# Experts from the second on: transposing the gathered rows by 32x32 blocks on VectorE after a shuffle by transfers, in place of TensorE transposes

## The reference

```python
gates = softmax(x_flat @ gating_w)                      # x_flat: 4096 x 256
topk_w, topk_idx = top_k(gates, 2)
norm_w = topk_w / (sum(topk_w) + 1e-8)
# each expert takes at most 1280 (token, choice) items, in order of tokens
buf[e, slot] = x_flat[token]                            # 8 x 1280 x 256
h = relu(einsum('ecd,edh->ech', buf, w1) + b1)          # hidden width 1024
out_e = einsum('ech,ehd->ecd', h, w2) + b2
out[token] += out_e[e, slot] * norm_w                   # for the items with a slot
x = layernorm(x + out)
```

## Time and profile before

| | us |
|---|---|
| median of 3 runs | 818.93 (818.16 to 819.34) |
| the profiled execution | 819.39 |
| its span, first to last instruction | 817.7 |
| TensorE busy (matmul) | 771.9 (94%) |
| VectorE busy | 605.5 (74%) |
| ScalarE busy | 442.8 (54%) |
| GpSimd busy | 403.4 (49%) |

### The profile page before, as it was taken

One profiled execution on the slowest core, in us unless ns is written; L12 is line 12 of the kernel. 1 busy time (PEld: TensorE's weight loads), 2 busy tenths in 40 slices (PEclk: granted clock), 3 DMA queues, 4 the chain that ended last, 5 costly groups with the idle time before them and its releaser, 6 DMA issues.

```text
span 817.7 us, 16633 instructions
## 1 busy us (share of the span) xinstructions
PE 771.9 (94%) x5919; PEld 644.4 (79%) x5919; DVE 605.5 (74%) x1325; ACT 442.8 (54%) x753; POOL 403.4 (49%) x599
## 2 busy tenths in 40 slices
PE   7789999999999988889999999999999999999993
PEld 6567777777777755778898898888988988988993
DVE  6657888889888898968657568568568567575982
ACT  3156777777777767645345345345445344444670
POOL 1000166665565547764364464463552553546774
PEclk9689999999999999999999999999999999999998
DMA  5567776565555682443352452452441633434841
GB/s 160 119 158 168 173 167 137 138 149 122 121 123 110 126 197 64 160 147 81 83 106 44 97 110 40 97 110 40 101 107 30 150 53 78 103 52 66 316 167 48
DMA packets 71534, 94.35 MB, mean 115 GB/s; under 512 B 10924, under 2 KB 55885, under 8 KB 71324
## 3 DMA queue, kind: packets, MB, share of 16 engines
q1 hardware_dynamic: 53308, 69.10, 32.1%
q0 software_dynamic: 16928, 22.61, 15.6%
q10 hardware_dynamic: 1216, 1.57, 0.9%
HBM read 39.76 MB, written 27.92 MB: 83 GB/s over the span
## 4 chain that ended last, share of the span: by engine, by line
PE 76%; DVE 12%; issue 4%; POOL 3%; DMA 3%; ACTq 0%; ACT 0%; POOLq 0%; DVEq 0%; SPq 0%
PE bank L1723 15%; PE bank L990 11%; DVE negm L895 10%; PE wide L1692 8%; PE wide L1691 8%; PE wide L1690 8%; PE bank L1725 8%; PE wide L1035 7%; PE bank L1669 2%; PE wide L1053 2%; PE bank L999 2%; PE bank L1100 1%; POOL slot_list L538 1%; DMA stack<-qk 1%; POOL out L1420 1%
## 5 line engine op out<-in xcount | busy, mean ns | idle before, releaser
L1364 POOL DMA_INDIRECT acc_rows<-o_w,lists x70 | 116.8, 1668 | 178.7 <-ACT o_w L1513 165.3
L895 DVE TENSOR_REDUCE negm<-wide 128x4 f32<-128x1024 f32 x128 | 156.1, 1222 | 36.8 <-PE wide L1035 36.7
L635 ACT ACTIVATE probs<-wide 128x1024 f32<-128x1024 f32 x128 | 131.0, 1024 | 61.8 <-PE wide L1053 60.2
L1480 ACT ACTIVATE h<-wide,b1T 128x512 f32<-128x512 f32 (+1 forms) x200 | 115.3, 601 | 89.2 <-PE wide L1692 65.2
L1725 PE MATMUL bank<-stack,h_lo 128*128 128x256 f32 x560 | 156.7, 280 | 0.0
L1690 PE MATMUL wide<-g_hi,stack 128*128 128x512 f32 (+1 forms) x400 | 139.4, 349 | 0.9 <-ACT h L1480 0.7
L1692 PE MATMUL wide<-g_hi,stack 128*128 128x512 f32 (+1 forms) x400 | 139.1, 348 | 0.0
L1691 PE MATMUL wide<-g_lo,stack 128*128 128x512 f32 (+1 forms) x400 | 138.9, 347 | 0.0
L1513 ACT ACTIVATE o_w<-o_b,lists 128x256 f32<-128x256 f32 x70 | 35.7, 510 | 147.5 <-DVE o_b L1651 147.5
L1723 PE MATMUL bank<-stack,h_hi 128*128 128x512 f32 x304 | 108.0, 399 | 1.6 <-DVE o_b L1651 1.6
L1725 PEld LDWEIGHTS bank<-stack,h_lo 128*128 128x128 f32 x560 | 105.9, 189 | 0.0
(11 more groups left out here) (212 smaller groups left out, 1637.9 us busy)
## 6 DMA issues: line engine op xcount, KB each, us to landing
stack<-qk SPq DMA_DIRECT2D x180, 128.0 KB, 3.9
w_raw<-in_L_ffn_w SPq DMA_DIRECT2D x16, 1024.0 KB, 5.9
x_sb<-in_L_attn_x SPq DMA_DIRECT2D x16, 256.0 KB, 4.7
x_rows<-x SPq DMA_DIRECT2D x16, 256.0 KB, 3.6
acc_rows<-x SPq DMA_DIRECT2D x16, 256.0 KB, 4.1
acc_sb<-acc_rows SPq DMA_DIRECT2D x8, 512.0 KB, 8.3
out<-acc_sb SPq DMA_DIRECT2D x8, 512.0 KB, 2.6
x_rows<-zrow SPq DMA_DIRECT2D x2, 1152.0 KB, 6.6
```

What stands on the lines that cost most here:

```text
L635: nc.scalar.activation(probs[:, i % 4].rearrange("p x c t -> p x (c t)"), shifted_banks(i)[:, :, :], ACT.Exp, scale=SCALE).then_inc(exp_do ...
L895: nc.vector.tensor_reduce(negm[n % 2][:, :, :, u].rearrange("p c x -> p x c"), score_banks(PAIRS * n + u)[:, :, :].rearrange("p x (c t) -> ...
L1364: nc.gpsimd.indirect_dma_start(out=acc_d, out_offset=bass.IndirectOffsetOnAxis(ap=lists[:, e, QC * c + r, 0:1], axis=0), in_=o_w[c][:, r, ...
L1480: ins = nc.scalar.activation(h[u % 2][:, t], banks[BZ[u % 4]][:, t], ACT.Relu, bias=b1T[:, FT * e + f:FT * e + f + 1])
```

## The change

From expert 1 on, TensorE transposes nothing. The rows of a group are first shuffled from SBUF to SBUF by 16 transfers that SP issues: the transfer (q, t) takes the 32 partitions of token block t, and of each row the 32 columns of column block q out of every 128, and puts them on the 32 partitions of block q. VectorE then turns all 32x32 blocks of a chunk in one transpose instruction (`turn`), and the copy into `g_hi` and the subtraction for `g_lo` read its result from SBUF. The 256 or 128 pieces of a transfer are of 128 bytes each.

SP's program now has, for each expert, the w2 load, the first and the second shuffle, the w1 load of the next expert, and the third shuffle. A shuffle waits for the gathers of its chunks and for the turning of the group two before it. A gather waits for the shuffle that last read its buffer. `AHEAD` goes from 5 to 6. In `expert_order` the taking in moves: chunks 0 and 1 after 5 of the 8 units of the third group's layer 1, chunk 2 after 4 of the 8 units of the first group's, chunks 3 and 4 between layer 2 of chunk 3 and of chunk 4 of the expert before (in the last expert, after layer 1 of its second group). To find room, part of `acc_sb` moves into the weights' raw buffers, and some semaphores are merged. Core of the diff:

```diff
-    AHEAD = 5
+    AHEAD = 6
+    BLOCK = 32
+    QUARTERS = P // BLOCK
+    MOVES = QUARTERS * QUARTERS
+    IN_WEIGHTS = 2
...
+        shuffled = [sb(f"shuffled{i}", [P, PAIR, QC * DK, QUARTERS, BLOCK]) for i in range(2)]
+        turned_rows = [sb(f"turned{i}", [P, QC * DK, P]) for i in range(2)]
...
+        def acc_group(i):
+            if i < 2 * IN_WEIGHTS:
+                raw = (w1_raw, w2_raw)[i // IN_WEIGHTS][:, :, :].rearrange("p x y -> p (x y)")
+                return raw.rearrange("p (i t d) -> p i t d", i=IN_WEIGHTS, t=GROUP)[:, i % IN_WEIGHTS]
+            return acc_sb[:, i - 2 * IN_WEIGHTS]
+        def moved_count(e, s):
+            return 16 * MOVES * ((super_no(e, s) - len(SUPERS)) // 2 + 1)
...
         def sync_program(sp):
-            for e in range(1, NE):
-                sp.wait_ge(gT_ready, NC * (e - 1) + 3)
+            def load_w1(e):
                 sp.wait_ge(w1_hi_done, PARTS * e)
                 sp.wait_ge(w1_lo_done, PARTS * e)
                 sp.dma_start(w1_raw[:, :, :], w1_d[e].rearrange("(c p) f -> p c f", p=P)).then_inc(w1_loaded, 16)
+            def load_w2(e):
                 sp.wait_ge(w2_hi_done, PARTS * e)
                 sp.wait_ge(w2_lo_done, PARTS * e)
                 sp.dma_start(w2_raw[:, :, :], w2_d[e].rearrange("(f p) d -> p f d", p=P)).then_inc(w2_loaded, 16)
+            def shuffle(e, s):
+                i, count = super_no(e, s), len(SUPERS[s])
+                for c in SUPERS[s]:
+                    sp.wait_ge(gathered[c], 16 * QC * (e + 1))
+                if i >= len(SUPERS) + 2:
+                    e_, s_ = divmod(i - 2, len(SUPERS))
+                    sp.wait_ge(turned, NC * (e_ - 1) + SUPERS[s_][-1] + 1)
+                src = rows_of[s][:, :, :, :].rearrange("p c r (k q b) -> p (c r k) q b", q=QUARTERS, b=BLOCK)
+                dst = shuffled[i % 2][:, 0:count].rearrange("p c x t b -> p (c x) t b")
+                for q, t in itertools.product(range(QUARTERS), repeat=2):
+                    sp.dma_start(dst[q * BLOCK:(q + 1) * BLOCK, :, t, :], src[t * BLOCK:(t + 1) * BLOCK, :, q, :]).then_inc(moved[i % 2], 16)
+            sp.wait_ge(gT_ready, 3)
+            load_w1(1)
+            for e in range(1, NE):
+                load_w2(e)
+                shuffle(e, 0)
+                shuffle(e, 1)
+                if e + 1 < NE:
+                    load_w1(e + 1)
+                shuffle(e, 2)
...
             def rows_hi(e, c):
                 s, off = of_chunk(c)
                 i = super_no(e, s)
-                act.wait_ge(gT_ready, NC * e + c + 1)
                 if i >= 2:
                     act.wait_ge(z_ready, unit_no(*divmod(i - 1, len(SUPERS)), 0, None))
+                if e > 0:
+                    act.wait_ge(turned, NC * (e - 1) + c + 1)
+                    nc.scalar.activation(chunk_view(g_hi, e, c), turned_view(e, c), ACT.Copy).then_inc(g_hi_done, 1)
+                    return
+                act.wait_ge(gT_ready, c + 1)
...
+            def turn(e, c):
+                s, off = of_chunk(c)
+                i, n = super_no(e, s), NC * (e - 1) + c
+                dve.wait_ge(moved[i % 2], moved_count(e, s))
+                if n >= 2:
+                    dve.wait_ge(g_hi_done, NC + n - 1)
+                    dve.wait_ge(g_lo_done, NC + n - 1)
+                nc.vector.transpose(turned_rows[(NC * e + c) % 2][:, :, :].rearrange("p x t -> p (x t)"),
+                                    shuffled[i % 2][:, off // C].rearrange("p x t b -> p (x t b)")).then_inc(turned, 1)
+            def take_in(e, chunks):
+                if e > 0:
+                    for c in chunks:
+                        turn(e, c)
+                for c in chunks:
+                    rows_lo(e, c)
...
@@ expert_order
         else:
             layer1(e, second)
-            take_in(e, 3)
-            take_in(e, 4)
+            if last:
+                take_in(e, (3, 4))
             layer2(e, 0)
             layer2(e, 1)
...
+        layer1(e, third, range(5))
+        take_in(e + 1, (0, 1))
+        layer1(e, third, range(5, 8))
+        if split_w1:
+            split_w1(e + 1)
         layer2(e, 2)
         if e + 1 < NE - 1:
-            layer1(e + 1, first)
-            take_in(e + 1, 2)
+            layer1(e + 1, first, range(4))
+            take_in(e + 1, (2,))
+            layer1(e + 1, first, range(4, 8))
         layer2(e, 3)
+        if e + 1 < NE - 1:
+            take_in(e + 1, (3, 4))
         layer2(e, 4)
-        if not last and split_w2:
+        if split_w2:
             split_w2(e + 1)
```

More of the change, by code:

```diff
@@ L119, in _ @@
         def _(pool):
-            gather, add_back = second[1](pool)
+            gather, add_back, rows_free = second[1](pool)
             first[1](pool, gather)
-            second[2](pool, gather, add_back)
+            second[2](pool, gather, add_back, rows_free)
         @block.scalar
@@ L1028, in scores @@
                     pe.wait_ge(wog_lo_done, 1)
[L1029 removed]
+                    pe.wait_ge(gate_copied, 2)
                 pe.wait_ge(max_done, max(i - 1, 0) if i < ALONE else i)
@@ L1232, in experts @@
         lists = sb("lists", [P, NE, BLK, ENTRY_WORDS], I32)
-        rows = [sb(f"rows{c}", [P, QC, D]) for c in range(2)]
+        rows_first = sb("rows_first", [P, 2, QC, D])
         h = [sb(f"h{i}", [P, WIDE]) for i in range(2)]
@@ L1236, in experts @@
         o_w = [sb(f"o_w{c}", [P, QC, D]) for c in range(NC)]
-        rows.append(sb("rows2", [P, QC, D]))
+        rows_second = sb("rows_second", [P, 1, QC, D])
         b2_all = sb("b2_all", [P, NE, D])
         g["b2_all"] = b2_all
-        rows += [sb(f"rows{c}", [P, QC, D]) for c in range(3, NC)]
+        rows_third = sb("rows_third", [P, 2, QC, D])
+        rows_of = (rows_first, rows_second, rows_third)
+        rows = [rows_of[s][:, i] for s, cs in enumerate(SUPERS) for i in range(len(cs))]
         low = [sb(f"low{r}", [P, D]) for r in range(QC)]
@@ L1366, in add_back, with gpsimd_program @@
                         in_=o_w[c][:, r, :], in_offset=None, compute_op=ALU.add).then_inc(added[c], 16)
-            return gather, add_back
-        def gpsimd_program(pool, gather, add_back):
+            return gather, add_back, rows_free
+        def gpsimd_program(pool, gather, add_back, rows_free):
             pool.wait_ge(g["late0_loaded"], 16)
-            for n in range(EC, AHEAD):
-                gather(n // NC, n % NC)
+            for c in range(EC, NC):
+                gather(0, c)
             pool.wait_ge(lists_loaded, 16)
             pool.wait_ge(late_loaded, 16)
+            for n in range(NC, AHEAD):
+                gather(n // NC, n % NC)
             def gather_sums(c):
-                pool.wait_ge(gT_ready, NC * LASTE + c + 1)
+                rows_free(LASTE, c)
                 for i in range(NC):
@@ L1730, in tensor_program, with take_in @@
         def tensor_program(pe, transposes, layer1, layer2):
-            expert_order(NE, transposes, layer1, layer2, None, None)
+            def take_in(e, chunks):
+                if e == 0:
+                    for c in chunks:
+                        transposes(0, c)
+            expert_order(NE, take_in, layer1, layer2, None, None)
         return (sync_program, gpsimd_steps, gpsimd_program, scalar_steps, scalar_program, vector_steps, vector_program,
```

101 lines of the change are left out of this document (60 added, 41 removed).

## The result

The changed kernel takes 841.81 us (median of 4 runs, 838.25 to 842.73), the kernel before 819.13 us on the same chip (818.16 to 820.72): a ratio of 1.0267, interval 1.0231 to 1.0302. The forecast was 827.6 us. The direction was right, the size was not: +22.7 us instead of +8.7. The profiled run takes 842.73 us with a span of 841.0.

The account below looks back on a forecast made before the run. TensorE was taken to bound the kernel, waiting for nothing in the experts. Six waits of 4.0 us less 15.3 us of transposes gave +8.7 us: 828.1 on the profiled run, 827.6 in terms of the median; range 804 to 844.

Parts of the forecast that it names:

- rival D: At layer 2 of chunk 0, each 2.9 us pause also costs 3.5 us of clock: 842 us; 0.20 with rival E.
- What the change takes away: 140 TensorE transposes in experts 1 to 7, 0.109 us each: 15.3 us less, an expert becomes 55.6 us.
- VectorE's and ScalarE's new work: One VectorE turn per chunk at 0.69 us, subtraction 0.69 as before; ScalarE's copy 0.65 us.
- rival E: VectorE's turn costs 1.22 us, total about 840, or 0.43 us, about 823; chance 0.20 together with rival D.
- The third shuffle: Lands at 39.9, for experts 1 to 6; TensorE waits 2.9 us at layer 2 of chunk 0, six times.
- B: Third shuffle hidden, at 0.38 us per transfer; only the 15.3 us saving remains: 803.6 us; chance 0.19.
- C: Third shuffle's burst goes at 0.50 us per transfer and lands 1.7 us late, six times: 813.8 us; chance 0.16.
- The 1.1 us for chunk 0's bank: TensorE wants the bank at 52.9, VectorE's chunk 0 bias ends at 54.0: 1.1 us more, six times.
- The wait for w1's split at 16.5: Before layer 1 of the next expert's first group, w1's first half is 0.1 us late, costed at nothing.
- The first shuffle has cover: It lands near 4.8, its turn comes at 9.0; with the later weighing about 2 us are left, no cost.
- The bias step that ends 1.2 us later: Chunk 2's bias on VectorE ends at 19.6 instead of 18.4, moving the add-back from 18.2 to 19.5.
- The closing stage at nothing: Shared buffers and merged semaphores in the closing stage cost nothing, hidden by layers 1 and 2 of expert 7.

Follow-up runs that it names:

- after: The changed kernel itself, with the whole change made to the kernel before: 841.81 us, ratio 1.0267.
- run 5: Against the changed kernel, TensorE again transposes chunks 0 and 1 of expert 1: 836.25 us.
- both of 6: Two runs against the changed kernel: expert 7's turns of chunks 3 and 4 moved forward, 843.86 us; expert 7's chunks transposed by TensorE again, 836.70 us.
- the first run of 6: Against the changed kernel, expert 7's turns of chunks 3 and 4 moved behind layer 1 of its first group: 843.86 us.
- run 7's second step: Changed kernel with AHEAD 7, TensorE transposing expert 1's chunks 0, 1 and expert 7's 3, 4; plus layer 2 moved earlier between experts 6 and 7: 806.41 us.

## Why the prediction was right and where it failed

The measured 841.8 us lies in the stated range, which was drawn around all the cases, and next to rival D's 842. That is luck: D reaches 842 with 3.5 us of work lost to the clock behind each of six pauses. In the profiled run the clock stayed full behind two of the six and took 1.7 us of work behind each of four; 11 us more come from what D, like the forecast, had at nothing: the closing part (6.2), a second pause in the first period (2.9) and the last period (1.9).

**What the change takes away**: right. 55.62 us where nothing is late, against 55.6.

**VectorE's and ScalarE's new work**: right. Lines of after (busy us, mean ns, idle before):

```profile
L1627 DVE STREAM_TRANSPOSE turned<-shuffled 128x512 f32<-128x512 f32 x35 | 23.2, 693 | 42.8 <-DMA shuffled<-rows_third 37.9 <-DMA shuffled<-rows_first 4.9
...
L1537 ACT ACTIVATE g_hi<-turned 128x512 fp32r<-128x512 f32 x35 | 21.6, 632 | 73.7 <-DVE turned L1627 62.1 <-PE wide L1785 11.5
```

0.693 against 0.69 and 0.632 against 0.65; rival E is out. The pace in the Trainium skill's "Vector Engine (DVE) Microarchitecture Reference", section 3.8, had given an estimate near 0.6 us; the measurement decides for 0.69.

**The third shuffle**: right in place and size: six pauses of 3.0 us in the mean against 2.9. From the first issue to the turn it is 13.1 us in the period shown, against 12.3, and the gather before it lands 0.4 earlier. B and C, which need 0.38 and 0.50 us an issue, are out: the bursts shown take 10.3 to 11.4 us for 16, and the one that holds the period shown takes 0.71 an issue, more than the 0.644 charged. The shuffle of the second group, with half the bytes and half the pieces, takes 10.26 where the first takes 10.52 (run 5's fence). So what is paid for is neither bytes nor pieces: back to back a transfer costs 0.65 us. The Trainium skill's "DMA: Bandwidth & Descriptors", Rules for kernel authors, has transfers under 64 KB pay mostly overhead, and these two bursts agree.

**The 1.1 us for chunk 0's bank**: mis-sized. It is 0.4 in each of the two periods with full clock, and nothing in the other three, in which the lower clock stretches the products and VectorE is in time. The wait for w1's split at 16.5, where no margin was left, came in two of the five and was 0.3 and 0.2 us.

**The clock**: put at nothing in the forecast, and at 3.5 us of work per pause in rival D; both are wrong. In after the clock stays full behind two of the five middle pauses, and is at 0.50 for 3.4 us behind three. Over the runs after, 5 and both of 6, the five middle periods with full clock last 59.4 to 59.7; the thirteen with 3.4 us of low clock last 60.2 to 61.2, 60.7 in the mean: some 1.0 us of the 1.7 us of work reaches the end. Three such periods are 3.2 of the middle's +3.7. Outside the middle it costs as well: 3.4 us of lower clock in the first period of after, and 5.9 us in its closing part. D's size came twice ahead of layer 2, behind pauses of 3.65 and 3.17 us in the first run of 6: 6.8 us of low clock, periods of 62.48 and 61.57.

**The first shuffle has cover**: failed in the first period. I had worked the cover out from the steady rhythm; there GpSimd has had a period's time for the gathers. In the first period three other chunks' gathers stand ahead of them, all behind one load of lists. The period is 4.2 us over the forecast: a pause of 2.87 us before layer 1, and behind the pause ahead of layer 2 up to 1.7 us of work lost to the clock, are most of it. In the steady rhythm the 2 us that were to be left are used up as well (two more waits of 1.5 us together): in the chain of the period shown the first group's gather takes 4.72 us to land, where I had charged the median of 2.9 from a row that also gives 7.0.

**The bias step that ends 1.2 us later**: I named it and followed it to the add-back only. Between experts 6 and 7 layer 2 of chunk 3 follows chunk 2 at once, and TensorE waits 1.3 us for that bank; with 0.3 us before layer 1 of expert 7's chunk 2 that is most of the 1.9 by which the last period misses, and run 7's second step gives back 1.5.

**The closing stage at nothing**: the largest failure, 6.2 us. I asked whether the loads into the shared buffers come late, and that was the wrong question: without turns in expert 7 the closing part is 40.86 us with those buffers. What failed is the cover that I did not look for: in the last expert VectorE has statistics between its splits and no slack, and its five subtractions became five turns and five subtractions there. The load of an engine was weighed at the middle's appointments and not at the end. Of the 6.2 us, 3.0 are TensorE's wait for the late relu and 3.0 the lower clock behind it.

## What to carry to other kernels

A wait on an in-order engine costs what stands behind it: before work on a transfer is placed in the order, ask for each period, the first and the last too, when it lands and who is queued behind its reader. Bursts of small transfers are priced by the issue and can be free if what they wait for (here a gather behind an add-back) is issued early enough. A cover worked out from the steady rhythm holds in the steady rhythm alone; the turn into it, the turn out of it and the closing stage each need their own look at the engine that gets the new work. And a pause of TensorE can cost more than its length: behind 16 of 22 pauses of about 3 us the clock fell for a while.

## What the runs showed of the hardware

Behind pauses of TensorE of nearly the same length the granted clock does different things. In after, run 5 and both of 6, layer 2 of chunk 0 waited for 2.69 to 3.69 us 22 times. Behind six of these pauses (2.76 to 3.06 us) the clock stayed full, behind fourteen (2.69 to 3.69 us) it was at the lower level for 3.4 us, and behind two (3.17 and 3.65 us) for 6.8 us. One pause of 2.97 us left it full and another did not; one of 3.65 us was followed by 3.4 us, another by 6.8. With 12 issues, a pause of 1.8 us left it full. With 20 issues, pauses of 4.19 and 4.46 us had 3.4, and pauses of 5.08, 5.33, 6.08 and 6.32 us had 6.8, a part of it in the pause itself, where it costs nothing. That TensorE falls back to the lower level after an idle stretch is in the Trainium skill's "TensorE: Matmul & The Clock Gate", Part 1, and these rows agree in kind. Why a pause of 3.03 us cost nothing and another of 2.81 us cost 1.7 us of work no run here shows.
